# Two transformer layers on one core: four sets of expert weights in the first layer instead of two, some loaded earlier, and a copy moved in VectorE's order

## The chip, the core and the metric

The kernel runs on one core of a Trainium2 chip. The core has five engines that run their own instruction lists and meet at semaphores: TensorE (PE in the profile; PEld is its loading of weights), VectorE (DVE), ScalarE (ACT), GpSimd (POOL) and SyncE (SP), which here only issues transfers (DMA). Transfers are carried out by 16 DMA engines between the chip's memory (HBM) and the core's SBUF. Products land in PSUM. The metric is the device time of one execution in microseconds, as the median over runs.

## The reference

The input is x, 8 sequences of 100 rows of 256 values, and a context of 8 times 361 rows of 192. Two layers are applied; each adds a cross attention and then a feed-forward part. All arithmetic is in float32. What matters here is the feed-forward part of the first layer, which sends every row to one of 8 experts:

```python
def _L0_ffn_ref(x, Wg, bg, W1, b1, W2, b2):      # D_MODEL 256, D_HIDDEN 1024, 8 experts
    gate_scores = softmax(einsum('btd,de->bte', x, Wg) + bg)
    top1_mask = one_hot(argmax(gate_scores), 8)
    top1_weight = sum(gate_scores * top1_mask)
    h = silu(einsum('btd,edh->bteh', x, W1) + b1)
    o = einsum('bteh,ehd->bted', h, W2) + b2
    return sum(o * top1_mask[..., None], axis=2) * top1_weight

x = x + L0_xattn(layernorm(x), ctx_768, ...)      # 16 heads
x = x + L0_ffn(layernorm(x), ...)                 # the experts of this case
x = x + L1_xattn(layernorm(x), ctx_768, mask, ...)
x = x + L1_ffn(layernorm(x), ...)                 # 64 experts, top 8, and a shared one
```

## The kernel before

The kernel is written without a scheduler: each engine has its own program, a list of functions called in order at the end of `build`, and semaphores named after what is ready (`w1_loaded`, `rows_used`, `ys_ready`) order them against each other. An engine takes its instructions in the order written; one that waits holds up all behind it on the same engine.

The stages are, in the time of the profile: projections of the first attention (to 72 us), the first attention (to 200), the gate of the first feed-forward (to 217), its experts (to 324), the second attention with its projections, and the second feed-forward, which fills the rest.

**The gate and the dispatch.** `pe_gate` and `dve_gate` pick an expert for each of the 800 rows and compute a slot for it, so that the rows of one expert lie together, in blocks of 128. `pool_dispatch` writes the rows to `xs_dram` in that order by eight indirect transfers (L944). There are eight experts and, with these inputs, eleven blocks: one expert has four blocks and each other has one.

**The experts.** Every engine walks over the blocks with `each_block`, a loop over pairs of experts (L981). Its body is written out for the two members of the pair, p = 0 and 1. For each expert it has three copies of the block's code: for the first block, for the second, and one in an inner loop for the third and further ones, whose turns are tested one by one. The numbers of blocks are read from `per_expert_i` into registers.

In one block (`block` in `pe_experts`) TensorE multiplies the 128 rows by W1 of the expert (L1040: 16 products in two passes, 32 matmuls), transposes the rows of the next block (L1031, `take_rows`), and multiplies the hidden layer by W2 (L1053). ScalarE applies the bias and silu (L1082) and loads the rows of later blocks. VectorE copies the transposed rows of the next block out of PSUM (L1098, `take_rows`), copies the bias of the next expert (L1103), and adds b2 (L1106). SP stores the block's result in `ys_dram` (L1011).

**The weights.** One expert's W1 and W2 are 1 MB each. `w1_e` and `w2_e` have two buffers each, all four in the memory of the attention's values (`vals_arena`). SP loads the sets of experts 0 and 1 in `sp_experts`, which stands behind `sp_load1_weights`; that waits until the first attention has added its last result (`A0.added`) and then loads context and weights for the second attention. From then on SP loads the set of expert e+1 into the other buffer once TensorE has begun expert e (`expert_begun`). In SP's program this stands behind the store of the block before.

**Entrance of the experts.** VectorE's `dve_experts` first takes the transposed biases b1 out of PSUM (L1111), clears a row (L1112), copies the first expert's bias (L1114), and then copies the first rows (`take_rows(0)`, L1098). ScalarE's first silu waits for L1114, TensorE's first product for L1098. At the same time GpSimd splits the second attention's weights in two instructions (L1202).

The hidden layer `hT` and the broadcast b2 lie in the memory of the attention's keys (`keys_arena`). The first attention uses the first 5,776 of its 13,032 columns.

Of the kernel before, what the change touches and what calls it, by code (L numbers as in the profile page):

```python
# [13 lines left out]
P = 128  # L14
# [13 lines left out]
def build(nc, a):  # L28
# [82 lines left out]
    w1_e = [carve(vals_arena, at_v, (2, H0)) for _ in range(2)]  # L111
    w2_e = [carve(vals_arena, at_v, (HC, D)) for _ in range(2)]
# [4 lines left out]
    hT = carve(keys_arena, at_k, (HC, P))  # L117
# [4 lines left out]
    b2_all = carve(keys_arena, at_k, (E0, D))  # L122
# [146 lines left out]
    w1_loaded = [sem(f"w1_loaded{p}") for p in range(2)]  # L269
    w2_loaded = [sem(f"w2_loaded{p}") for p in range(2)]  # L270
# [703 lines left out]
    def each_block(e, run):  # L974

        def within(n):
            return nc.s_assert_within(n, 0, NBLK - 1, skip_runtime_bounds_check_because=
                                      "all experts take NBLK blocks at most")

        e.wait_ge(slots_ready, 1)  # L980
        with e.Fori(0, E0 // 2) as i:  # L981
            for p in range(2):
                blocks = e.value_load(per_expert_i[0:1, 0, bass.ds(2 * i + p, 1)], min_val=1, max_val=MAXB)
                first = e.value_load(per_expert_i[0:1, 1, bass.ds(2 * i + p, 1)], min_val=0, max_val=NBLK - 1)
                run(first, i, p, True)
                with e.If(blocks > 1):
                    run(within(first + 1), i, p, False)
                    with e.If(blocks > 2):
                        with e.Fori(2, MAXB) as k:
                            with e.If(blocks > k):  # L990
                                run(within(first + k), i, p, False)

    def sp_experts(sp):
        sp.dma_start(b1_rows[:, :], a["L0_ffn_b1"].rearrange("e (m q) -> (e m) q", q=P)).then_inc(biases_loaded, 16)
        sp.dma_start(b2_all[:, :, :], a["L0_ffn_b2"].rearrange("(o e) d -> o e d", o=1).broadcast_to([P, E0, D])
                     ).then_inc(biases_loaded, 16)
        def load(e, p):
            sp.dma_start(w1_e[p], a["L0_ffn_W1"].rearrange("e (c q) h -> q (e c) h", q=P)[:, bass.ds(2 * e, 2), :]
                         ).then_inc(w1_loaded[p], 16)
            sp.dma_start(w2_e[p], a["L0_ffn_W2"].rearrange("e (m q) d -> q (e m) d", q=P)[:, bass.ds(HC * e, HC), :]  # L1000
                         ).then_inc(w2_loaded[p], 16)

        def block(n, i, p, first):
            if first:

                with sp.If(i > 0 if p == 0 else i < E0 // 2 - 1):
                    sp.wait_ge(expert_begun, 2 * i + p + 1)
                    load(nc.s_assert_within(2 * i + p + 1, 1, E0 - 1, skip_runtime_bounds_check_because=
                                            "after the last expert there is none to load"), 1 - p)
# [3 lines left out]
        load(0, 0)  # L1013
        load(1, 1)
# [12 lines left out]
    def pe_experts(pe):  # L1027
# [6 lines left out]
        def block(n, i, p, first):  # L1034
# [12 lines left out]
            if first:  # L1047
                pe.wait_ge(w2_loaded[p], 16 * i + 16)
            pe.wait_ge(ys_ready, n + 1)
            for m in range(HC):  # L1050
                if m % 4 == 0:
                    pe.wait_ge(hidden_ready, 2 * n + 1 + m // 4)
                last = nc.tensor.matmul(ys_ps, hT[:, m, :], w2_e[p][:, m, :], start=(m == 0), stop=(m == HC - 1))  # L1053
# [18 lines left out]
    def act_experts(act):  # L1072
# [3 lines left out]
        def block(n, i, p, first):  # L1076
            if first:
                act.wait_ge(b1_ready, 2 * i + p + 2)
            for half in range(2):
                act.wait_ge(hidden_in_psum, 2 * n + half + 1)  # L1080
                for m in range(4 * half, 4 * half + 4):
                    last = nc.scalar.activation(hT[:, m, :], hid_ps[half][:, m % 4, :], ACT.Silu,  # L1082
                                                bias=b1_col[p][:, m:m + 1])
# [11 lines left out]
    def dve_experts(dve):  # L1095
# [4 lines left out]
        def block(n, i, p, first):  # L1100
            take_rows(n + 1)
            if first:
                nc.vector.tensor_copy(b1_col[1 - p], b1_all[:, bass.ds(2 * i + p + 1, 1), :]).then_inc(b1_ready, 1)  # L1103
            dve.wait_ge(ys_in_psum, n + 1)
            dve.wait_ge(ys_stored, 16 * n + 16)
            nc.vector.tensor_tensor(ys_rows, ys_ps, b2_all[:, bass.ds(2 * i + p, 1), :].rearrange("p e d -> p (e d)"),  # L1106
                                    ALU.add).then_inc(ys_ready, 1)

        dve.wait_ge(b1_in_psum, 1)
# [6 lines left out]
        take_rows(0)  # L1116
# [914 lines left out]
    with nc.Block() as block:  # L2031
        @block.sync
        def _(sp):
# [3 lines left out]
            sp_load_moe(sp)  # L2037
            sp_load1_weights(sp)
# [101 lines left out]
```

## Time and profile before

| | us |
|---|---|
| median of 3 runs | 796.9 (794.32 to 797.54) |
| profiled execution: span of its records | 799.0 |
| time around that span | not given |
| TensorE busy in the span | 702.9 (88%) |
| ScalarE busy | 413.8 (52%) |
| VectorE busy | 372.2 (47%) |
| GpSimd busy | 253.4 (32%) |
| SP's queue (q1): 58.40 MB | 23.6% of 16 engines' span |

The median is over unprofiled runs, the span is that of one profiled execution, and here it is the longer of the two. A line of the timeline gives the start, the time from the first to the last of the instructions merged in it, the engine, the line of the kernel, and in square brackets how long the engine had been idle before it and what ended that. SPq and ACTq are transfers being issued. Names of tiles are those of the memory they lie in: the experts' weights read `v_all`, their rows, hidden layer and biases `kT_all`.

### The profile page before, as it was taken

The numbers are of one execution on the slowest core, as the hardware profiler recorded it, in microseconds if no ns is written. First come the engines' busy times: TensorE is split into PE (matmuls) and PEld (weight loads), VectorE is DVE, ScalarE is ACT, GpSimd is POOL, SyncE is SP. The second block draws the span as 40 slices with busy tenths as digits, with TensorE's granted clock in tenths as the row PEclk, the third lists the DMA queues.
The fourth block names the chain that finished last, engine by engine and source line by source line (L and its number), as shares of the span: only waits on it lengthen the run. The fifth ranks groups of instructions, "written<-read, shape, count | busy, mean of one in ns | idle before, by whom it ended". The sixth has DMA issues, their size and how long they took to land.

```text
span 799.0 us, 15926 instructions
## 1 busy us (share of the span) xinstructions
PE 702.9 (88%) x4979; PEld 569.5 (71%) x4980; DVE 372.2 (47%) x1126; ACT 413.8 (52%) x966; POOL 253.4 (32%) x322
## 2 busy tenths in 40 slices
PE   3997999997539999699999899986799999999995
PEld 2775666665438898477666566655479999999995
DVE  4223577776421111476777555556843434242432
ACT  2445789987313332355556878763234444444442
POOL 5112455553160000211211000001236666666652
PEclk9998799999559999899999999996899999999999
DMA  5126000000835971100100100000044443344431
GB/s 134 42 82 199 1 2 2 2 3 1 295 119 182 301 247 33 54 24 19 38 19 0 46 2 1 2 1 1 0 132 131 129 120 122 121 122 120 129 112 41
DMA packets 58549, 62.51 MB, mean 78 GB/s; under 512 B 5920, under 2 KB 51206, under 8 KB 58378
## 3 DMA queue, kind: packets, MB, share of 16 engines
q1 hardware_dynamic: 55530, 58.40, 23.6%
q10 hardware_dynamic: 1952, 1.91, 0.8%
q0 software_dynamic: 1024, 1.64, 0.7%
q8 instruction: 25, 0.41, 0.2%
q14 instruction: 18, 0.15, 0.1%
HBM read 54.72 MB, written 7.22 MB: 78 GB/s over the span
## 4 chain that ended last, share of the span: by engine, by line
PE 68%; DVE 11%; ACT 9%; issue 5%; DMA 3%; POOL 3%; SPq 1%; DVEq 0%; POOLq 0%; ACTq 0%
PE psum L1876 6%; PE psum L1878 6%; PE psum L1877 5%; ACT probs L697 4%; PE psum L1040 4%; PE psum L1053 3%; PE psum L1395 3%; PE psum L1891 3%; PE psum L1892 3%; PE psum L545 3%; PE psum L1890 3%; PE psum L559 3%; PE psum L1416 3%; PE psum L636 3%; PE psum L1403 2%
## 5 line engine op out<-in xcount | busy, mean ns | idle before, releaser
L2000 DVE TENSOR_TENSOR kT_all<-kT_all 128x400 f32<-128x400 f32 x60 | 36.6, 611 | 114.5 <-ACT kT_all L1934 106.5
L1973 POOL TENSOR_TENSOR h_low<-v_all,h_high 128x400 fp32r<-128x400 f32 x60 | 63.1, 1051 | 65.5 <-ACT h_high L1938 65.4
L1876 PE MATMUL psum<-xT_high,we_high 128*128 128x400 f32 x240 | 83.3, 347 | 0.0
L1878 PE MATMUL psum<-xT_high,we_low 128*128 128x400 f32 x240 | 82.8, 345 | 0.0
L1877 PE MATMUL psum<-xT_low,we_high 128*128 128x400 f32 x240 | 82.5, 344 | 0.0
L697 ACT ACTIVATE probs<-probs,negmax 100x361 f32<-100x361 f32 x128 | 68.9, 587 | 10.8 <-POOL probs L742 10.7
L1964 POOL TENSOR_TENSOR we_low<-v_all,we_high 128x512 fp32r<-128x512 f32 (+1 forms) x61 | 66.6, 1101 | 19.6 <-ACT we_high L1923 16.0
L750 DVE TENSOR_SCALAR_CACHE_REDUCE probs<-psum 100x361 f32<-100x361 f32 x128 | 60.7, 531 | 19.5 <-PE psum L626 19.5
L636 PEld LDWEIGHTS psum<-ident,probs 100*128 100x128 f32 (+1 forms) x384 | 40.2, 159 | 27.6 <-issue 19.8
L636 PE MATMUL psum<-ident,probs 100*128 100x100 f32 (+1 forms) x384 | 48.7, 266 | 11.1 <-ACT probsT L705 4.8
L1934 ACT ACTIVATE kT_all<-psum 128x400 f32<-128x400 f32 x60 | 30.0, 501 | 52.7 <-PE psum L1878 52.7
L1082 ACT ACTIVATE kT_all<-psum,kT_all 128x128 f32<-128x128 f32 x88 | 25.2, 369 | 52.1 <-PE psum L1040 52.1
L742 POOL TENSOR_SCALAR probs<-probs 100x722 f32<-100x722 f32 x64 | 50.4, 788 | 5.0
L1040 PE MATMUL psum<-kT_all,v_all 128*128 128x128 f32 x352 | 44.4, 287 | 7.0 <-DMA v_all<-in_L_ffn_W_dram 2.8
L1040 PEld LDWEIGHTS psum<-kT_all,v_all 128*128 128x128 f32 x352 | 43.1, 202 | 9.7 <-issue 5.9
L1938 ACT ACTIVATE h_high<-v_all 128x400 fp32r<-128x400 f32 x60 | 32.2, 536 | 30.3 <-DVE v_all L2005 30.3
L1876 PEld LDWEIGHTS psum<-xT_high,we_high 128*128 128x128 f32 x240 | 45.1, 188 | 0.5 <-DVE v_all L2005 0.2
L1877 PEld LDWEIGHTS psum<-xT_low,we_high 128*128 128x128 f32 x240 | 45.2, 188 | 0.2
L1878 PEld LDWEIGHTS psum<-xT_high,we_low 128*128 128x128 f32 x240 | 45.1, 188 | 0.0
L950 POOL TENSOR_TENSOR ctxT_low<-ctxT_full,ctxT_high 96x722 fp32r<-96x722 f32 x9 | 15.4, 1709 | 88.6 <-ACT ctxT_high L1070 88.6
L1891 PE MATMUL psum<-h_high,we_high 128*128 128x400 f32 x120 | 41.4, 345 | 0.0
L1892 PE MATMUL psum<-h_low,we_high 128*128 128x400 f32 x120 | 41.3, 344 | 0.0
(350 smaller groups left out, 1566.7 us busy)
## 6 DMA issues: line engine op xcount, KB each, us to landing
v_all<-in_L_ffn_W_dram SPq DMA_DIRECT2D x16, 1024.0 KB, 7.7
kT_all<-coefT_dram SPq DMA_DIRECT2D x30, 400.0 KB, 3.5
v_all<-in_L_ffn_Wg_dram SPq DMA_DIRECT2D x31, 128.0 KB, 2.1
v_all<-in_L_ffn_Wu_dram SPq DMA_DIRECT2D x31, 128.0 KB, 2.2
v_all<-in_L_ffn_Wd_dram SPq DMA_DIRECT2D x31, 128.0 KB, 2.1
ctx_nat<-in_ctx_dram SPq DMA_DIRECT2D x17, 192.0 KB, 2.5
xs_dram<-zeros SPq DMA_DIRECT2D x1, 2048.0 KB, 7.7
ys_dram<-zeros SPq DMA_DIRECT2D x1, 1792.0 KB, 12.5
```

Source lines behind the costliest of these rows:

```text
L636: last = nc.tensor.transpose(pT_ps[0:rows[t], t, hh * NQ:(hh + 1) * NQ], probs[:, n % NPB, hh, t * P:t * P + rows[t]], ident[0:NQ, 0:NQ])
L697: last = nc.scalar.activation(row, row, ACT.Exp, bias=negmax[:, n % NPB, hh:hh + 1])
L742: nc.gpsimd.tensor_scalar(pair, pair, CLAMP, -CLAMP, ALU.min, ALU.max).then_inc(A0.clamped, 1)
L750: last = nc.vector.tensor_scalar(probs[:, n % NPB, hh, 0:NKV], psum[0:NQ, n % 2 * 2 + hh, 0:NKV], -CLAMP, None, ALU.max, ALU.max, accum_ou ...
L1040: last = nc.tensor.matmul(hid_ps[m // 4][:, m % 4, :], w1_e[p][:, c, m * P:(m + 1) * P], xsT[:, c, :], start=(c == 0), stop=(c == 1))
L1876: nc.tensor.matmul(ps, we_high[p][:, col], xT_high[:, c, tok], start=(c == 0), stop=False)
L1877: nc.tensor.matmul(ps, we_high[p][:, col], xT_low[:, c, tok], start=False, stop=False)
L1878: last = nc.tensor.matmul(ps, we_low[p][:, col], xT_high[:, c, tok], start=False, stop=(c == 1))
L1891: nc.tensor.matmul(ps, we_high[p][:, col], h1_high[p][:, tok], start=False, stop=False)
L1892: last = nc.tensor.matmul(ps, we_high[p][:, col], h1_low[p][:, tok], start=False, stop=False)
L1964: nc.gpsimd.tensor_tensor(we_low[p][:, cols], we[p][:, cols], we_high[p][:, cols].bitcast(F32), ALU.subtract).then_inc(we_split, 1)
L1973: nc.gpsimd.tensor_tensor(h1_low[p][:, tok], h1T[:, tok], h1_high[p][:, tok].bitcast(F32), ALU.subtract).then_inc(h1_ready, 1)
```

## The change

The weights get four sets of buffers (`BUFS0`). Two W1 and one W2 lie in the upper part of the keys' memory, which the first attention leaves unused; the others lie in the memory of the values. W2 is loaded in two halves. The hidden layer and b2 move to the memory of the queries. W1 and W2 of expert 0 and W1 of expert 1 are loaded by `sp_load_first_experts`, ahead of SP's wait for the end of the first attention; the second half of expert 1's set and the sets of experts 2 and 3 are loaded behind it. When expert e has begun, SP loads the set of expert e+3. The loop over the experts has a body for four experts and two turns. In `dve_experts`, `take_rows(0)` is the first instruction.

```diff
-    w1_e = [carve(vals_arena, at_v, (2, H0)) for _ in range(2)]
-    w2_e = [carve(vals_arena, at_v, (HC, D)) for _ in range(2)]
+    BUFS0, KT0 = 4, 2 * B * NKV
+    queries_arena = qT_all[:, :]
+    at_t, at_q = [KT0], [0]
+    w1_e = [carve(keys_arena, at_t, (2, H0)) for _ in range(2)]
+    w2_e = [[carve(keys_arena, at_t, (HC // 2, D)) for _ in range(2)]]
+    w1_e += [carve(vals_arena, at_v, (2, H0)) for _ in range(2)]
+    w2_e += [[carve(vals_arena, at_v, (HC // 2, D)) for _ in range(2)] for _ in range(2)]
+    w2_e.append([carve(vals_arena, at_v, (HC // 2, D)), vals_arena[:, 6 * SLOT_V + 2048:8 * SLOT_V].rearrange(
+        "p (m d) -> p m d", m=HC // 2)])
...
-    hT = carve(keys_arena, at_k, (HC, P))
...
-    b2_all = carve(keys_arena, at_k, (E0, D))
+    b2_all = carve(queries_arena, at_q, (E0, D))
+    assert at_k[0] <= KT0 and at_v[0] <= 6 * SLOT_V and at_t[0] <= 4 * (B + 1) * (NKV + 1)
...
-        with e.Fori(0, E0 // 2) as i:
-            for p in range(2):
-                blocks = e.value_load(per_expert_i[0:1, 0, bass.ds(2 * i + p, 1)], min_val=1, max_val=MAXB)
-                first = e.value_load(per_expert_i[0:1, 1, bass.ds(2 * i + p, 1)], min_val=0, max_val=NBLK - 1)
+        with e.Fori(0, E0 // BUFS0) as i:
+            for p in range(BUFS0):
+                blocks = e.value_load(per_expert_i[0:1, 0, bass.ds(BUFS0 * i + p, 1)], min_val=1, max_val=MAXB)
+                first = e.value_load(per_expert_i[0:1, 1, bass.ds(BUFS0 * i + p, 1)], min_val=0, max_val=NBLK - 1)
...
+    def load_w1(sp, e, p):
+        sp.dma_start(w1_e[p], a["L0_ffn_W1"].rearrange("e (c q) h -> q (e c) h", q=P)[:, bass.ds(2 * e, 2), :]
+                     ).then_inc(w1_loaded[p], 16)
+
+    def load_w2(sp, e, p):
+        src = a["L0_ffn_W2"].rearrange("e (m q) d -> q (e m) d", q=P)
+        for half in range(2):
+            sp.dma_start(w2_e[p][half], src[:, bass.ds(HC * e + half * (HC // 2), HC // 2), :]).then_inc(w2_loaded[p], 16)
+
+    def sp_load_first_experts(sp):
+
+        load_w1(sp, 0, 0)
+        load_w2(sp, 0, 0)
+        load_w1(sp, 1, 1)
+
     def sp_experts(sp):
+        load_w2(sp, 1, 1)
         sp.dma_start(b1_rows[:, :], a["L0_ffn_b1"].rearrange("e (m q) -> (e m) q", q=P)).then_inc(biases_loaded, 16)
         sp.dma_start(b2_all[:, :, :], a["L0_ffn_b2"].rearrange("(o e) d -> o e d", o=1).broadcast_to([P, E0, D])
                      ).then_inc(biases_loaded, 16)
         def load(e, p):
-            sp.dma_start(w1_e[p], a["L0_ffn_W1"].rearrange("e (c q) h -> q (e c) h", q=P)[:, bass.ds(2 * e, 2), :]
-                         ).then_inc(w1_loaded[p], 16)
-            sp.dma_start(w2_e[p], a["L0_ffn_W2"].rearrange("e (m q) d -> q (e m) d", q=P)[:, bass.ds(HC * e, HC), :]
-                         ).then_inc(w2_loaded[p], 16)
+            load_w1(sp, e, p)
+            load_w2(sp, e, p)
 
         def block(n, i, p, first):
             if first:
 
-                with sp.If(i > 0 if p == 0 else i < E0 // 2 - 1):
-                    sp.wait_ge(expert_begun, 2 * i + p + 1)
-                    load(nc.s_assert_within(2 * i + p + 1, 1, E0 - 1, skip_runtime_bounds_check_because=
-                                            "after the last expert there is none to load"), 1 - p)
+                with sp.If(i > 0 if p == 0 else i < E0 // BUFS0 - 1):
+                    sp.wait_ge(expert_begun, BUFS0 * i + p + 1)
+                    load(nc.s_assert_within(BUFS0 * i + p + BUFS0 - 1, BUFS0, E0 - 1, skip_runtime_bounds_check_because=
+                                            "after the last expert there is none to load"), (p - 1) % BUFS0)
             sp.wait_ge(ys_ready, n + 2)
             sp.dma_start(ys_dram[bass.ds(n * P, P), :], ys_rows).then_inc(ys_stored, 16)
 
-        load(0, 0)
-        load(1, 1)
+        for e in (2, 3):
+            load(e, e)
         each_block(sp, block)
...
-                pe.wait_ge(w2_loaded[p], 16 * i + 16)
+                pe.wait_ge(w2_loaded[p], 32 * i + 32)
...
-                last = nc.tensor.matmul(ys_ps, hT[:, m, :], w2_e[p][:, m, :], start=(m == 0), stop=(m == HC - 1))
+                last = nc.tensor.matmul(ys_ps, hT[:, m, :], w2_e[p][m // 4][:, m % 4, :], start=(m == 0), stop=(m == HC - 1))
...
-                act.wait_ge(b1_ready, 2 * i + p + 2)
+                act.wait_ge(b1_ready, BUFS0 * i + p + 2)
...
-                nc.vector.tensor_copy(b1_col[1 - p], b1_all[:, bass.ds(2 * i + p + 1, 1), :]).then_inc(b1_ready, 1)
+                nc.vector.tensor_copy(b1_col[1 - p % 2], b1_all[:, bass.ds(BUFS0 * i + p + 1, 1), :]).then_inc(b1_ready, 1)
...
+        take_rows(0)
         dve.wait_ge(b1_in_psum, 1)
         dve.wait_ge(biases_loaded, 32)
         nc.vector.tensor_copy(b1_all[:, 0:E0, :], b1_ps.rearrange("p (e m) -> p e m", e=E0))
...
         dve.sem_inc(ys_stored, 16)
-        take_rows(0)
         each_block(dve, block)
...
             sp_load_moe(sp)
+            sp_load_first_experts(sp)
             sp_load1_weights(sp)
             sp_experts(sp)
```

SP's program between the zero fills (L828) and the loop over the experts (L981), before: `ctx` is the context and `L1_xattn` the second attention's weights, ahead of them SP waits for the attention's end.

```order
L828 DMA ys_dram<-zeros 128x14x256
L429 DMA ctx_nat0<-in_ctx_768_dram 128x2x192
...
L1151 DMA early<-in_L1_xattn_Wq_dram 128x2x512
L994 DMA kT_all<-in_L0_ffn_b1_dram 64x128
L995 DMA kT_all<-in_L0_ffn_b2_dram 128x2048
L998 DMA v_all<-in_L0_ffn_W1_dram 128x2x1024
L1000 DMA v_all<-in_L0_ffn_W2_dram 128x8x256
L998 DMA v_all<-in_L0_ffn_W1_dram 128x2x1024
L1000 DMA v_all<-in_L0_ffn_W2_dram 128x8x256
L981 UNCONDITIONAL_BRANCH
```

The same stretch of SP's program, in the changed kernel:

```order
L836 DMA ys_dram<-zeros 128x14x256
L1002 DMA kT_all<-in_L0_ffn_W1_dram 128x2x1024
L1008 DMA kT_all<-in_L0_ffn_W2_dram 128x4x256 x2
L1002 DMA kT_all<-in_L0_ffn_W1_dram 128x2x1024
L437 DMA ctx_nat0<-in_ctx_768_dram 128x2x192
...
L1173 DMA early<-in_L1_xattn_Wq_dram 128x2x512
L1008 DMA v_all<-in_L0_ffn_W2_dram 128x4x256 x2
L1018 DMA kT_all<-in_L0_ffn_b1_dram 64x128
L1019 DMA qT_all<-in_L0_ffn_b2_dram 128x2048
L1002 DMA v_all<-in_L0_ffn_W1_dram 128x2x1024
L1008 DMA v_all<-in_L0_ffn_W2_dram 128x4x256 x2
...
L989 UNCONDITIONAL_BRANCH
```

Four loads (3 MB) now stand ahead of the wait and seven (5 MB, the last two like the two before them) behind it, where four of 1 MB each stood.

VectorE's program from the gate's last instruction to the loop over the experts, before:

```order
L907 CAST slot<-slot_f 100x8
L1111 COPY kT_all<-psum 128x64
L1112 MEMSET kT_all 128x8
L1114 COPY kT_all<-kT_all 128x8
L1098 COPY kT_all<-psum 128x256
L981 UNCONDITIONAL_BRANCH
```

And in the changed kernel:

```order
L915 CAST slot<-slot_f 100x8
L1120 COPY kT_all<-psum 128x256
L1134 COPY kT_all<-psum 128x64
L1135 MEMSET kT_all 128x8
L1137 COPY kT_all<-kT_all 128x8
L989 UNCONDITIONAL_BRANCH
```

The copy of the first rows (L1098, now L1120) has moved ahead of the three instructions on the biases; nothing else on VectorE changes its place.

## Rows read from the trace of the kernel before

**Rows 1.** Busy time by stretch; columns: length, engines' busy us, PEclk, DMA share, GB/s.
```profile
core 0: us, PE busy (x) PEld busy (x) DVE busy (x) ACT busy (x) POOL busy (x), PEclk, DMA share, GB/s
...
74.00:82.00 8.00, 5.37 (x28) 2.92 (x28) 3.93 (x17) 5.31 (x11) 4.03 (x8) 0.50 0.01 2
201.00:223.00 22.00, 10.20 (x58) 9.50 (x56) 7.44 (x31) 7.28 (x11) 4.81 (x5) 0.50 0.96 324
...
239.00:240.00 1.00, 1.00 (x8) 1.00 (x8) 0.00 (x0) 0.02 (x1) 0.00 (x0) 0.62 0.00 0
...
248.00:297.00 49.00, 45.61 (x306) 41.35 (x306) 6.00 (x19) 18.41 (x55) 0.00 (x0) 1.00 0.87 289
```

**Rows 2.** Timeline of TensorE, the first products of blocks (start, length).
```profile
234.06 6.54 PE L1040 MATMUL psum<-kT_all,v_all 128*128 128x128 f32 x32 [2.22 <-DVE kT_all L1098]
...
244.11 3.77 PE L1040 MATMUL psum<-kT_all,v_all 128*128 128x128 f32 x32
...
269.26 3.84 PE L1040 MATMUL psum<-kT_all,v_all 128*128 128x128 f32 x32 [1.08 <-DMA v_all<-in_L_ffn_W_dram]
...
277.33 3.81 PE L1040 MATMUL psum<-kT_all,v_all 128*128 128x128 f32 x32 [0.55 <-DMA v_all<-in_L_ffn_W_dram]
...
292.30 3.73 PE L1040 MATMUL psum<-kT_all,v_all 128*128 128x128 f32 x32
...
299.55 3.73 PE L1040 MATMUL psum<-kT_all,v_all 128*128 128x128 f32 x32
...
315.99 3.81 PE L1040 MATMUL psum<-kT_all,v_all 128*128 128x128 f32 x32 [1.79 <-issue]
```

**Rows 3.** The chain that ended last, 226 to 330 us.
```profile
247.64 0.42 SPq L998
248.27 8.83 DMA v_all<-in_L_ffn_W_dram
...
264.34 4.88 DMA v_all<-in_L_ffn_W_dram
```

**Rows 4.** Timeline of all engines where the experts begin.
```profile
226.26 0.99 POOL L944 DMA_INDIRECT xs_dram<-kT_all,slot  x1 [0.31 <-issue]
...
228.93 3.29 ACTq L1074 DMA_DIRECT2D kT_all<-xs_dram  x2
228.93 2.34 POOL L1202 TENSOR_TENSOR wk_low<-v_all,wk_high 96x1024 fp32r<-96x1024 f32 x1
...
229.51 0.23 DVE L1111 COPY kT_all<-psum 128x64 f32<-128x64 f32 x1 [12.88 <-PE psum L1061]
...
229.78 3.82 DVE L1114 COPY kT_all<-kT_all 128x8 f32<-128x8 f32 x1
...
231.15 0.69 PE L1031 MATMUL psum<-ident,kT_all 128*128 128x128 f32 x2 [1.68 <-DMA kT_all<-xs_dram]
231.23 2.34 POOL L1202 TENSOR_TENSOR wv_low<-v_all,wv_high 96x1024 fp32r<-96x1024 f32 x1
233.52 0.41 DVE L1098 COPY kT_all<-psum 128x256 f32<-128x256 f32 x1
234.02 1.28 ACT L1082 ACT_TABLE_LOAD   x1 [14.43 <-DVE kT_all L1114]
...
237.88 1.14 ACT L1082 ACTIVATE kT_all<-psum,kT_all 128x128 f32<-128x128 f32 x4 [2.58 <-PE psum L1040]
...
241.19 0.16 DVE L1103 COPY kT_all<-kT_all 128x8 f32 x1
```

**Rows 5.** Transfers from 256 to 325 us: queues, then issues.
```profile
q1 hardware_dynamic: 7736, 11.56, 50.2%
q10 hardware_dynamic: 1296, 1.18, 5.5%
...
kT_all<-xs_dram ACTq DMA_DIRECT2D x9, 128.0 KB, 5.4
```

**Rows 6.** Transfers from 234 to 256 us: the instruction queue.
```profile
q8 instruction: 2, 0.03, 0.6%
```

More of the change, by code:

```diff
@@ L116, in build @@
     xsT = carve(keys_arena, at_k, (2, P))
-    hT = carve(keys_arena, at_k, (HC, P))
+    hT = carve(queries_arena, at_q, (HC, P))
     ys_rows = carve(keys_arena, at_k, (D,))
@@ L268, in build @@
     xs_loaded, ys_in_psum, ys_stored = sem("xs_loaded"), sem("ys_in_psum"), sem("ys_stored")
-    w1_loaded = [sem(f"w1_loaded{p}") for p in range(2)]
-    w2_loaded = [sem(f"w2_loaded{p}") for p in range(2)]
+    w1_loaded = [sem(f"w1_loaded{p}") for p in range(4)]
+    w2_loaded = [sem(f"w2_loaded{p}") for p in range(4)]
     xsT_ready = sem("xsT_ready")
@@ L1082, in block @@
                     last = nc.scalar.activation(hT[:, m, :], hid_ps[half][:, m % 4, :], ACT.Silu,
-                                                bias=b1_col[p][:, m:m + 1])
+                                                bias=b1_col[p % 2][:, m:m + 1])
                 last.then_inc(hidden_ready, 1)
@@ L1102, in block @@
             if first:
-                nc.vector.tensor_copy(b1_col[1 - p], b1_all[:, bass.ds(2 * i + p + 1, 1), :]).then_inc(b1_ready, 1)
+                nc.vector.tensor_copy(b1_col[1 - p % 2], b1_all[:, bass.ds(BUFS0 * i + p + 1, 1), :]).then_inc(b1_ready, 1)
             dve.wait_ge(ys_in_psum, n + 1)
             dve.wait_ge(ys_stored, 16 * n + 16)
-            nc.vector.tensor_tensor(ys_rows, ys_ps, b2_all[:, bass.ds(2 * i + p, 1), :].rearrange("p e d -> p (e d)"),
+            nc.vector.tensor_tensor(ys_rows, ys_ps, b2_all[:, bass.ds(BUFS0 * i + p, 1), :].rearrange("p e d -> p (e d)"),
                                     ALU.add).then_inc(ys_ready, 1)
+        take_rows(0)
         dve.wait_ge(b1_in_psum, 1)
```

## The prediction, made before the changed kernel was run

> **What bounds the kernel now.** I read the page's slices first, then a table of stages, then the stretch from 196 to 323 us instruction by instruction, then the chain of waits. Reference times are those of the trace before the change, in us from the start of the span.
>
> The table of stages [rows 1] shows three things. The transfer engines stand still in the first attention (share 0.01 from 74 to 82). They are full right behind it (0.96 from 201 to 223, at 324 GB/s), while TensorE is busy with the gate for 10.20 of 22.00 us at a granted clock of 0.50, that is 1.2 GHz. And in the experts (248 to 297) TensorE is busy 45.61 of 49.00 us at the full clock with the transfers at 0.87 beside it. So TensorE bounds the experts, and what is to be had there is its idle time.
>
> How much that is comes from the starts of the blocks of 128 rows, each of which opens with the 32 matmuls of L1040 [rows 2]. Where no weights are loaded a block takes 299.55 - 292.30 = 7.25 us. From 244.11 to 292.30 there are six blocks in 48.19 us, and six clean ones are 43.50: 4.69 us are lost. The chain of waits says to what: it runs through the weights' transfers before experts 2, 4 and 6 [rows 3] (a third one, of the same length as the second, stands before expert 6). The reason stands in the code. With two sets, the set of expert e+1 can be loaded only once expert e has begun and SP has stored the block before it.
>
> One more gap, 1.79 us before 315.99 [rows 2], is called issue. It follows the only expert with four blocks, whose inner loop still has three empty turns to test. The change keeps that loop, so I keep the gap.
>
> The other loss is at the entrance [rows 4]. The first 128 rows land, TensorE transposes them from 231.15 to 231.84, and VectorE copies the result only at 233.52. It was in the bias copy L1114 from 229.78 for 3.82 us. A copy of the same shape takes 0.16 at 241.19. What ends when L1114 ends (233.60) is GpSimd's second subtraction (231.23 + 2.34 = 233.57): the two shared something, and the small copy stood behind it.
>
> **The change, part by part.**
>
> *Rows ahead of the biases.* In VectorE's program the copy of the rows moves ahead of L1111, L1112 and L1114. It waits for the transposes alone, which end at 231.84, 1.68 us ahead of its start now. With a little for the handover it gains 1.6. Would GpSimd hold this copy too? Its source is PSUM. The nearest row is L1111, also from PSUM, which took 0.23 us at 229.51 beside the first subtraction [rows 4]. It has 64 columns instead of 256, so the bounds are 0 (held like L1114) and 1.6; I take 1.6. The bias copies then end as before at about 233.6, because GpSimd sets that. What is late next: ScalarE waits for them, then loads its table (1.28 us, from 0.42 after L1114's end), so it is ready at 235.3. The first half of the hidden layer now comes 3.82 us (237.88 - 234.06) after 232.46, at 236.3. So the table is hidden, with 1.0 us to spare.
>
> By the Trainium skill (SBUF — State Buffer, Who interferes with whom), GpSimd holds the port pair that it shares with VectorE for a whole instruction, and a VectorE instruction with at most one SBUF input outside the 2-port modes never wants it. By that rule the gain is the full 1.6; had the copy read SBUF it would be 0.
>
> *The clock at that place.* The first block ran at 0.50 until about 239.8 (the slice from 239 to 240 has 0.62, [rows 1]). Its 32 matmuls took 6.54 against 3.73 at the full clock [rows 2]; at 0.50 all the way they are 7.46. If the clock rises as long after the start as before, 5.7 us, the whole 1.6 stays. If it rises at the same instant, the matmuls take from 232.46 to 239.8 and not to 240.6, and 0.8 stays. If it rises after some 4 us, the matmuls take 4.0 + (7.46 - 4.0)/2 = 5.7, and 2.4 are gained. I take 1.6.
>
> *Four sets of weights.* The waits in the six blocks go if the weights are there in time. Sets 0 to 3 are all asked for before the experts begin, sets 4 to 7 when experts 1 to 4 begin. Expert 1 would begin at about 242.5, and SP gets to its load 3.5 us behind that (247.64 against 244.11 before, [rows 2, 3]), at 246.0. The set needs 9.5 us from there (248.27 + 8.83 = 257.10, less 247.64), so set 4 is there at 255.5; expert 4 starts three blocks after expert 1, at 264.3. Sets 5 and 6 follow a block apart. From 248 to 297 six sets with their rows took 0.87 of 49 us [rows 1], 7.1 us each, so they just keep up with 7.25. The gain is the 4.69 less what is no wait for weights: a loop that turns back once instead of three times still has to read its registers. The matmuls behind such a turn take 3.84 and not 3.73 at 269.26 and 299.55 [rows 2]; I leave 0.2 for the one turn. Bounds: 4.7 above; below, 3.8, if what the chain doesn't name stays: 0.82 before 277.33 (277.33 - 269.26 - 7.25) and 0.1 behind expert 6's start. I take 4.5, since the 0.82 lies in the first block of a set too.
>
> *One and a half sets loaded early.* SP's program now has four loads (3 MB) behind the zero fills and ahead of its wait for the attention's end; SP has nothing else there, so nobody waits for SP. The transfers would fill 74 to 83 us, where the engines were at 0.01. What could they slow down? In the experts L1040 took 3.73 beside full transfers at 292.30 and 3.73 at 299.55 beside none, and 3.81 to 3.84 behind a gap [rows 2]. So 0, with 0.5 as the upper bound (3% of the eight us, twice).
>
> *Two and a half sets behind the attention.* Before, 4 MB of expert weights went there, now 5 MB. The extra MB takes 3.2 us at 324 GB/s. The transfers run full until 223 [rows 1], now until about 226. SP issues them later too, but is first wanted at 245. The biases, now behind half a set, still land long ahead of 229.51, where VectorE takes them. The scatter of the rows on GpSimd ends at 227.25 and shares the engines. Its last piece is issued at 226.26, when the extra MB is nearly through, and the reading of the rows starts at 228.93 [rows 4]. Cost between 0 and 3.2; I take 0.3, near the end at which GpSimd's own issue sets the pace.
>
> *hT and b2 in the queries' memory, weights of the second layer in two halves:* same instructions and sizes. The buffers are free there since the first attention is over. 0.
>
> *Code.* The loop over the experts has four bodies and two turns instead of two and four. In 234 to 256 the trace has 2 instruction transfers, and in 256 to 325 none, though the loop turned back twice [rows 5, 6]. So code that was there stays there. I take 0, for the new bodies too, which are reached by jumps forward like the second body in the first turn: no gap before 244.11.
>
> **Sum.** 1.6 + 4.5 - 0.3 = 5.8 us, all of it on the chain, since the chain leaves the experts through the last block's store and gather. Against the profiled execution: 799.0 - 5.8 = 793.2 for the span. What lies around its span is not shown, and the median of the runs, 796.9, is even below the span, so I take the difference from the median: 791.1 us.
>
> **Rivals.**
>
> *Code, on the slower side.* The gap of 1.79 is not the loop's tests but the fetch of the next expert's code, and with double the code every change of expert pays it. For it: the gap is called issue, and it stands at a jump to another copy. Against it: at 244.11 such a jump costs nothing, and no instruction transfer stands in 256 to 325 [rows 5, 6]. It would be 6 further gaps, 10.7 us, less the 5.8: 796.9 + 4.9 = 801.8. It turns the sum from the fourth gap on.
>
> By the Trainium skill (Runtime: NRT & Kernel Launch, Instruction fetch mechanics) a taken branch whose target is outside a window of two pages stalls until the page is fetched; it puts pages at 16 KiB. By that rule this rival would be the forecast. The trace does not agree as far as two bodies go, since the turns in 256 to 325 fetched nothing; for four bodies no row shows it.
>
> *The waits come back.* The loads of sets 4 to 6 press on the engines together with the rows (5.4 us to landing there, [rows 5]) and the block stores behind them in SP's queue, and TensorE waits about 1 us in each of four blocks: 796.9 - 5.8 + 4 = 795.1. Against it: the transfers have a slack of nine us on set 4, and some four on set 6.
>
> *Only the waits go.* GpSimd holds the new first copy as well: 796.9 - 4.2 = 792.7.
>
> **How the numbers follow.** Forecast 0.66, with a range of its own from 788.5 to 793.5: the clock's instant gives 0.9 either way, the scatter up to 1.5, and further falls and rises of the clock behind the experts shift with the work. Only the waits 0.12; the waits come back 0.13; code 0.06; 0.03 is left for the rest. A measurement here tells 0.5% (4 us, about the 3.2 between the three runs) from no change. Faster than 792.9 is most of the forecast and half of "only the waits": 0.66. Within 0.5%: 0.28. Slower: 0.06. The range 787.5 to 796.5 leaves out the code and the far ends.
>
> **What would show it.** Right: the copy of the rows starts within 0.1 us of the transposes' end, no matmul of the experts waits for a transfer, blocks are 7.25 us apart from the second to the seventh, and the stage ends at about 317 instead of 323.1. The first attention lasts as before, with the transfers full from 74 to 83. Wrong: waits called issue at experts 2, 3 or 4 with instruction transfers beside them (code), the first copy held until 233.5, the reading of the first rows more than a microsecond behind GpSimd's last scatter (the extra MB), or weights in the chain again.

## The result, and the profile after

The changed kernel takes 802.6 us, the median of 4 runs (802.12 to 803.3), against 796.4 for the kernel before on the same chip: a ratio of 1.0081, with a 95% interval from 1.0065 to 1.0096. It is slower by 6.2 us, where 5.8 us were to be gained. Its profiled execution took 803.0 us with a span of 801.0 us, so some 2.0 us lie around a span. The profiled execution of before had a span of 799.0 us: with as much around it, that execution was a long one, some 4.6 us above its median. Spans of the two are therefore not compared below; stretches inside the experts are.

The starts of the blocks on TensorE (L1062, which was L1040) answer to [rows 2]. The columns are start, length, engine, line, tiles, and in brackets the idle time before it.

```profile
232.70 6.63 PE L1062 MATMUL psum<-kT_all 128*128 128x128 f32 x32 [1.35 <-DVE kT_all L1120]
...
242.84 3.76 PE L1062 MATMUL psum<-kT_all 128*128 128x128 f32 x32
...
250.11 1.28 PE L1062 MATMUL psum<-kT_all,v_all 128*128 128x128 f32 x10
253.96 2.61 PE L1062 MATMUL psum<-kT_all,v_all 128*128 128x128 f32 x22 [2.57 <-issue]
...
265.55 5.60 PE L1062 MATMUL psum<-kT_all,v_all 128*128 128x128 f32 x32 [5.30 <-issue]
...
275.00 3.83 PE L1062 MATMUL psum<-kT_all 128*128 128x128 f32 x32 [0.17 <-issue]
...
289.58 3.73 PE L1062 MATMUL psum<-kT_all,v_all 128*128 128x128 f32 x32
...
296.83 3.73 PE L1062 MATMUL psum<-kT_all,v_all 128*128 128x128 f32 x32
```

No wait for weights is left, as predicted. In their place stand a gap of 2.57 us inside the block of expert 2 and one of 5.30 us ahead of expert 3, both called issue. From 242.84 to 296.83 six blocks take 53.99 us, and six clean ones 43.50: 10.49 us are lost, where it was 4.69. From 289.58 on the blocks are 7.25 us apart.

The chain of waits (start, us, what) answers to [rows 3]: it goes through the gaps.

```profile
251.39 2.57 issue
...
260.25 5.30 issue
```

The long gap has a second price. These are busy times by stretch, with the columns of [rows 1]. After the gap TensorE ran its 32 matmuls in 5.60 us and not 3.73, with a granted clock of 0.50, that is 1.2 GHz. TensorE had been idle since 260.25, and the clock was already at 0.50 in the stretch from 262.5.

```profile
253.00:262.00 9.00, 6.29 (x40) 5.52 (x39) 0.93 (x3) 2.29 (x8) 0.00 (x0) 1.00 0.90 299
262.50:269.00 6.50, 3.46 (x16) 3.48 (x17) 0.00 (x0) 0.00 (x0) 0.00 (x0) 0.50 0.18 32
270.00:276.00 6.00, 5.83 (x38) 5.07 (x37) 0.93 (x3) 2.91 (x7) 0.00 (x0) 1.00 0.79 279
```

The transfers of instructions answer to [rows 6]. First from 240 to 275 us, and then in the two gaps alone, 251 to 254 and 260.3 to 265.6 (queue: packets, MB, share):

```profile
q8 instruction: 5, 0.08, 1.0%
...
q8 instruction: 1, 0.02, 2.2%
...
q8 instruction: 2, 0.03, 2.8%
q14 instruction: 2, 0.02, 0.9%
```

Five pieces of 0.016 MB are fetched in the first turn of the loop, where two were before; one lies in the short gap and two in the long one. From 275 to 325 us q8 moves nothing. That q8 carries TensorE's code is seen in the runs below: where TensorE's program alone is changed, the count on q8 changes with it. The long gap also has two small transfers on q14; the gap of 8.80 us in the kernel with unused code, below, has none on q14, so such a gap does not need them.

The entrance, on all engines, answers to [rows 4]:

```profile
224.92 0.99 POOL L952 DMA_INDIRECT xs_dram<-kT_all,slot  x1 [0.30 <-issue]
...
228.56 3.18 ACTq L1096 DMA_DIRECT2D kT_all<-xs_dram  x2
...
230.66 0.69 PE L1053 MATMUL psum<-ident,kT_all 128*128 128x128 f32 x2 [2.53 <-DMA kT_all<-xs_dram]
...
231.39 0.42 DVE L1120 COPY kT_all<-psum 128x256 f32<-128x256 f32 x1 [16.10 <-PE psum L1053]
```

The copy starts right behind the transposes, as it should. But the first product comes at 232.70, 0.89 us after the copy's end: from the transposes' start to it are 2.04 us instead of 2.91, so 0.87 us are gained, not 1.6. And ScalarE reads the rows 3.64 us after the last scatter's start, where it was 2.67; the transposes start 5.74 us after it, where it was 4.89.

### The profile page after: what moved, and what is told of

The parts are those of the page before. It is cut to its first block, busy times and chain, and to the rows that moved or that the text cites. A ratio compares the mean times of both kernels' runs of the same rounds, so it can differ in the third digit from the quotient of the medians.

```text
span 801.0 us, 15892 instructions
## 1 busy us (share of the span) xinstructions
PE 701.8 (88%) x4979; PEld 570.0 (71%) x4980; DVE 367.4 (46%) x1126; ACT 411.3 (51%) x964; POOL 253.7 (32%) x322
## 4 chain that ended last, share of the span: by engine, by line
PE 69%; DVE 11%; ACT 9%; issue 5%; POOL 2%; DMA 1%; DVEq 0%; POOLq 0%; ACTq 0%; SPq 0%
PE psum L1062 6%; PE psum L1898 6%; PE psum L1900 5%; PE psum L1899 5%; PE psum L1075 5%; ACT probs L705 4%; PE psum L553 3%; PE psum L1913 3%; PE psum L1914 3%; PE psum L1912 3%; PE psum L567 3%; PE psum L1417 3%; PE psum L1438 2%; PE psum L1425 2%; PE psum L644 2%
## 5 line engine op out<-in xcount | busy, mean ns | idle before, releaser
L705 ACT ACTIVATE probs<-probs,negmax 100x361 f32<-100x361 f32 x128 | 68.9, 587 | 10.3 <-POOL probs L750 10.0
L1104 ACT ACTIVATE qT_all<-psum,kT_all 128x128 f32<-128x128 f32 x88 | 25.2, 369 | 62.7 <-PE psum L1062 62.7
L1912 PE MATMUL psum<-h_high,we_low 128*128 128x400 f32 x120 | 41.1, 343 | 0.0
L1800 POOL TENSOR_TENSOR xT_low<-kT_all,xT_high 128x1600 fp32r<-128x1600 f32 x1 | 3.6, 3559 | 118.7 <-ACT xT_high L1779 118.7
```

Source lines behind the costliest of these rows:

```text
L705: last = nc.scalar.activation(row, row, ACT.Exp, bias=negmax[:, n % NPB, hh:hh + 1])
L1912: nc.tensor.matmul(ps, we_low[p][:, col], h1_high[p][:, tok], start=False, stop=False)
```

## The experiments

What is compared throughout: the time; "lost", which is what six blocks from the second block's start take above 43.50 us; and "scatter to read", from the start of GpSimd's last scatter to the start of ScalarE's reading of the rows.

**The kernel before, once more.**

> The kernel before, profiled once more: a control, with no edit. Its first profiled execution had a span of 799.0 us and its own time some 4.6 us above the median of its timed runs. Theory A (that execution was an unlucky one, by the phase of the clock in attention): the span is now 793 to 796 us, and the waits for weights (six blocks, 4.69 us in all) are there again within 1 us. Theory B (a profiled execution always costs this): the span is 798 to 800 us again.

It took 793.9 us with a span of 792.1 us. Six blocks went from 240.79 to 288.90 us, 4.61 us lost, and scatter to read took 2.69. The span is that of theory A, and the two stretches repeat within 0.1 us, so the first profile's long span is not theirs. That the clock in the attention made it long was not followed up. From the first transposes to the first product it was 3.09 us here, against 2.91 in the first profile.

**VectorE's rows first, alone.**

```diff
+        take_rows(0)
         dve.wait_ge(b1_in_psum, 1)
...
-        take_rows(0)
         each_block(dve, block)
```

> The kernel before with one edit: the copy of the first rows stands ahead of the bias copies on VectorE. The trace of the changed kernel shows the copy starting right behind its transposes, but the first expert product only 2.04 us after the transposes began, with 0.88 us called issue behind the copy. Theory F (a new floor: TensorE's own register reads of the loop take that long after the transposes): the first product starts 2.04 us after the transposes began, where before it was 2.91, so the stage gains 0.9 us and the median 0.5 to 1.2. Theory P (the prediction's term): 1.6 us, with the product 1.3 us behind the transposes. Rival: the extra weights had delayed TensorE in the changed kernel, not the register reads; then the product starts within 1.4 us here too.

It took 795.1 us (12 runs), a ratio of 0.9984 with an interval from 0.9967 to 1.0001. From its timeline of TensorE and VectorE:

```profile
228.82 0.69 PE L1031 MATMUL psum<-ident,kT_all 128*128 128x128 f32 x2 [1.67 <-DMA kT_all<-xs_dram]
230.96 5.94 PE L1040 MATMUL psum<-kT_all,v_all 128*128 128x128 f32 x32 [1.44 <-DVE kT_all L1098]
...
229.55 0.42 DVE L1098 COPY kT_all<-psum 128x256 f32<-128x256 f32 x1 [15.24 <-PE psum L1031]
...
230.16 1.14 DVE L1115 COPY kT_all<-kT_all 128x8 f32<-128x8 f32 x1
```

The first product comes 2.14 us behind the transposes' start, though the copy is done 1.17 us behind it. In both kernels with the new order some 0.9 to 1.0 us lie between the copy's end and the product. In that place TensorE's program has only the entry into the loop, with its register reads; this says where the time is, and no run took the reads away. The bias copy again ends with GpSimd's second subtraction (231.30 and 231.26), which hurts nobody now. The edit is worth 0.8 to 0.95 us (against 2.91 and 3.09 in the two profiles of before), too little for the timed runs to show beyond doubt.

**Code that never runs, in the kernel before.** Three more copies of the block's code stand at the end of each of TensorE's two bodies, under a condition that is never true. TensorE has about as much loop code as in the changed kernel; buffers, loads and order are those of before.

```diff
+                if unused:
+                    with e.If(blocks > MAXB - 1):
+                        for _ in range(unused):
+                            run(first, i, p, False)
...
-        each_block(pe, block)
+        each_block(pe, block, unused=3)
```

> The kernel before, two sets and two bodies, with three more copies of a block's code in TensorE's program at the end of each body, under a test (more than 6 blocks) that is never true here. Nothing more is executed but the test. Theory C (the gaps of the changed kernel are the first fetch of code that a jump lands in): the second body now begins about twice as far behind the first, so a gap called issue of 2.5 to 5.5 us stands at expert 1 for the first time, with an instruction transfer beside it, none from expert 2 on, and the kernel is 2 to 7 us slower. Theory T (the gaps come from the registers and tests of a four-body loop, or from the weights): no gap there, and a time within 1 us of before.

It took 810.4 us, a ratio of 1.0171 (1.0138 to 1.0204): 14.2 us slower than before, by code that does nothing. Its timeline of TensorE:

```profile
245.44 3.81 PE L1044 MATMUL psum<-kT_all,v_all 128*128 128x128 f32 x32 [2.92 <-issue]
...
261.72 5.37 PE L1044 MATMUL psum<-kT_all,v_all 128*128 128x128 f32 x32 [8.80 <-issue]
...
270.64 3.81 PE L1044 MATMUL psum<-kT_all,v_all 128*128 128x128 f32 x32
...
326.29 5.43 PE L1044 MATMUL psum<-kT_all,v_all 128*128 128x128 f32 x32 [2.01 <-issue]
```

Its transfers of instructions, from 238 to 262 us and in the long gap alone (252.9 to 261.7):

```profile
q8 instruction: 5, 0.08, 1.2%
...
q8 instruction: 3, 0.05, 2.1%
```

Five pieces again, three of them in the gap of 8.80 us: 2.93 us each. One of the other two lies in the gap of 2.92 us. From 262 to 325 us there is none, and no such gap at the later experts; only the gap behind the expert with four blocks is 2.01 us, and 32 matmuls behind it take 5.43 us where they took 3.81 before. That code costs was expected, and the gap at expert 1 too. The size (2 to 7 us) was not, because a gap of 8.80 us stands at expert 2 as well, where the loop turns back for the first time and none was expected. The six blocks lose 13.44 instead of 4.69 us; with 2.92 ahead of them and 1.62 behind the last gap that is 13.3 of the 14.2 us.

**The loop's code walked over before it is needed.** The changed kernel with one more turn of TensorE's loop ahead of the first rows; in it every expert is jumped over.

```diff
+        with e.Fori(0, E0 // BUFS0 + 1) as t:
+            for p in range(BUFS0):
+                with e.If(t > 0):
...
+            with e.If(t < 1):
+                entry()
```

> The changed kernel, with one turn more of the loop in TensorE's program, run while TensorE waits for the scatter: in it a test at each body's start jumps over the body, so that the places where the bodies begin are touched once; the first rows are transposed at its end. Theory C: the gaps of 2.57 us in expert 2 and 5.30 us before expert 3, and the 1.87 us that the fallen clock cost behind them, go for the most part, the instruction transfers move to 217 to 230 us, and the kernel takes 7 to 10 us less than the changed one, about 793 to 795. If only the first page of each body is touched and the later ones are still missing, the gap of 2.57 inside expert 2's products stays. Theory T: the gaps stay where they are, and the time is that of the changed kernel, 802.6.

It took 795.9 us (10 runs), 0.9985 of before (0.9963 to 1.0006), and 6.8 us less than the changed kernel, just under the 7 to 10 that were expected. Its transfers of instructions from 217 to 234 us, and then its timeline of TensorE:

```profile
q8 instruction: 5, 0.08, 2.3%
```

```profile
232.73 0.34 PE L1109 MATMUL psum<-ident,kT_all 64*128 64x64 f32 x1 [16.11 <-issue]
...
235.46 5.25 PE L1087 MATMUL psum<-kT_all 128*128 128x128 f32 x32 [1.77 <-issue]
...
251.52 3.73 PE L1087 MATMUL psum<-kT_all,v_all 128*128 128x128 f32 x32
...
258.77 3.73 PE L1087 MATMUL psum<-kT_all,v_all 128*128 128x128 f32 x32
...
312.24 5.46 PE L1087 MATMUL psum<-kT_all,v_all 128*128 128x128 f32 x32 [1.88 <-issue]
```

All five pieces now come before the experts, q8 moves nothing from 234 to 325 us, and 0.74 us of the six blocks are lost instead of 10.49. That it only draws level with before has its reason in the first row, for the most part: the walk holds TensorE until 232.73, and the first product comes 2.8 us later than in the changed kernel. The last row adds 1.65 us: behind the gap of 1.88 us the 32 matmuls take 5.46 us, where they take 3.81 behind the changed kernel's 1.79.

**Two copies of the block's code instead of three.** The changed kernel; on TensorE the second block of an expert goes through the inner loop too.

```diff
                 with e.If(blocks > 1):
-                    run(within(first + 1), i, p, False)
-                    with e.If(blocks > 2):
-                        with e.Fori(2, MAXB) as k:
+                        with e.Fori(1, MAXB) as k:
```

> The changed kernel, with two instead of three copies of the block's code in each of TensorE's four bodies (the second block of an expert is run by the inner loop as well). The jump from one body to the next passes over one copy instead of two. Theory C: shorter jumps land in code that is nearer, so the 5.30 us before expert 3 shrink to 2.6 or less and the clock does not fall there; the time is 3 to 8 us under the changed kernel's 802.6. Theory T (tests and registers): one more turn of tests for each expert with more than one block, no gain, 802.6 or a little more.

It took 792.3 us (8 runs), a ratio of 0.9945 (0.9922 to 0.9967): faster than before, and 10.3 us under the changed kernel, more than the 3 to 8 expected. In its timeline of TensorE nothing waits from the second block to the eighth, be it for weights or for code:

```profile
242.91 3.75 PE L1067 MATMUL psum<-kT_all 128*128 128x128 f32 x32
...
250.19 3.81 PE L1067 MATMUL psum<-kT_all,v_all 128*128 128x128 f32 x32
...
257.51 3.73 PE L1067 MATMUL psum<-kT_all,v_all 128*128 128x128 f32 x32
...
264.96 3.83 PE L1067 MATMUL psum<-kT_all 128*128 128x128 f32 x32
...
286.80 3.73 PE L1067 MATMUL psum<-kT_all,v_all 128*128 128x128 f32 x32
```

0.39 us of the six blocks are lost, of which 0.20 lie at the loop's turn (257.51 to 264.96 is 7.45). Three pieces of code still come from 240 to 275 us, and nothing waits for them:

```profile
q8 instruction: 3, 0.05, 0.6%
```

The entrance is worse than in the changed kernel, though nothing was changed there (GpSimd's and ScalarE's rows): scatter to read is 4.61 us. Why it is longer than the changed kernel's 3.64, with the same transfers asked for, stays open.

```profile
224.79 0.99 POOL L952 DMA_INDIRECT xs_dram<-kT_all,slot  x1 [0.30 <-issue]
...
229.40 3.21 ACTq L1101 DMA_DIRECT2D kT_all<-xs_dram  x2
```

**Two sets of buffers, one and a half loaded early.** The changed kernel with `BUFS0` = 2 and without the loads of sets 2 and 3 ahead of the loop. It keeps the new places in memory, the early loads and the new order.

```diff
-    BUFS0, KT0 = 4, 2 * B * NKV
+    BUFS0, KT0 = 2, 2 * B * NKV
...
-        for e in (2, 3):
-            load(e, e)
```

> The changed kernel, but with two sets of weights buffers instead of four; the early loads and VectorE's rows first stay. Expected by the theory (turns that land on code not yet loaded cost 9.7 us, four sets gain 4.7): no bodies for the third and fourth set, so no gap of 2.6 or 5.3 us at experts 1 and 2; the waits for weights of the kernel before come back (4 to 5 us in six blocks); first product 2.1 us behind the row transposes' start; 794 to 796 us, 7 us below the changed kernel. Rival (the memory layout or the early loads themselves slow something): 798 us or more with no gap at the experts' turns.

It took 797.2 us (10 runs), 0.9992 of before (0.9972 to 1.0012). No gap called issue is left at experts 1 to 6, and the waits for weights are back:

```profile
250.54 3.84 PE L1060 MATMUL psum<-kT_all 128*128 128x128 f32 x32 [1.14 <-DMA kT_all<-in_L_ffn_W_dram]
...
255.91 3.72 PE L1073 MATMUL psum<-kT_all,qT_all 128*128 128x256 f32 x16 [1.32 <-DMA kT_all<-in_L_ffn_W_dram]
...
268.00 3.84 PE L1060 MATMUL psum<-kT_all 128*128 128x128 f32 x32 [1.13 <-DMA kT_all<-in_L_ffn_W_dram]
```

The six blocks lose 5.55 us and not 10.49. The median lies 5.4 us below the changed kernel and 1 us above what was expected; its interval reaches that. So the early loads by themselves gain nothing: what limits two sets is the loading of the next expert's.

**How much is queued behind the attention.** Two kernels, both with two copies of the code. In the first, set 3 is asked for when expert 0 has begun, and 3 MB of expert weights stand behind the attention instead of 5. In the second, nothing is loaded early, and it is 8 MB.

```diff
-        for e in (2, 3):
-            load(e, e)
+        load(2, 2)
...
-                with sp.If(i > 0 if p == 0 else i < E0 // BUFS0 - 1):
+                with sp.If(i < (E0 // BUFS0 if p == 0 else E0 // BUFS0 - 1)):
```

```diff
-            sp_load_first_experts(sp)
             sp_load1_weights(sp)
+            sp_load_first_experts(sp)
```

> The kernel of e4_two_copies (two copies of the block's code, 792.3 us) with the fourth set's first load put to expert 0's beginning, so that less is queued behind the attention while GpSimd's scatter and ScalarE's read of the rows go on. Theory D (the extra traffic delays the rows by 1 to 2 us): the rows are read 1.5 to 2.5 us after the last scatter's issue instead of 3.6, and the time falls to 790 to 791 us. Rival (that delay is by chance, or the fourth set comes too late for expert 3): 792 to 793 us, or a new wait at expert 3's first block.

> The kernel of e4_two_copies, but the first one and a half sets are loaded behind the attention too, so that four whole sets (8 MB) are queued there instead of 5. Theory D: the weights' traffic lasts some 9 us longer, the rows are read 4 us or more after the last scatter's issue, and the first expert's weights, which are first in their queue, still come in time; 793.5 to 797 us. Rival (the queued megabytes don't matter to the scatter and the rows): the same 792.3 us as e4_two_copies within 0.7 us.

They took 790.5 us (6 runs; ratio 0.9913, 0.9887 to 0.9939) and 797.8 us (10 runs; 0.9999, 0.9978 to 1.0020). The first lies in its expected range, though the rows are read 2.69 us behind the last scatter and not 1.5 to 2.5; the second lies 0.8 us above its range. ScalarE's reading and the transposes with 3 MB (the last scatter started at 224.41):

```profile
227.10 3.06 ACTq L1100 DMA_DIRECT2D kT_all<-xs_dram  x2
...
229.08 0.69 PE L1057 MATMUL psum<-ident,kT_all 128*128 128x128 f32 x2 [1.46 <-DMA kT_all<-xs_dram]
```

And with 8 MB (the last scatter started at 224.37):

```profile
230.48 6.58 ACTq L1101 DMA_DIRECT2D kT_all<-xs_dram  x2
...
235.99 0.69 PE L1058 MATMUL psum<-ident,kT_all 128*128 128x128 f32 x2 [8.41 <-DMA kT_all<-xs_dram]
```

All kernels side by side; the DMA share is that of the 2.7 us from the last scatter's start:

| kernel | MB behind attention | DMA share | scatter to read, us | lost in six blocks, us | time, us |
|---|---|---|---|---|---|
| before | 4 | 0.27 | 2.67 | 4.69 | 796.4 |
| before again | 4 | 0.27 | 2.69 | 4.61 | 793.9 |
| rows first | 4 | 0.29 | 2.69 | 5.07 | 795.1 |
| unused code | 4 | 0.26 | 2.69 | 13.44, and 2.92 ahead | 810.4 |
| two sets | 1 | 0.26 | 2.68 | 5.55 | 797.2 |
| changed | 5 | 0.71 | 3.64 | 10.49 | 802.6 |
| walked first | 5 | 0.73 | 5.02 | 0.74 | 795.9 |
| two copies | 5 | 0.77 | 4.61 | 0.39 | 792.3 |
| two copies, set 3 later | 3 | 0.26 | 2.69 | 0.37 | 790.5 |
| two copies, none early | 8 | 1.04 | 6.11 | 0.38 | 797.8 |

Up to 4 MB the rows are read 2.67 to 2.69 us behind the last scatter in every kernel; with 5 MB it is 3.6 to 5.0 us, and with 8 MB 6.1. With 8 MB the rows also take longer to arrive: the transposes start 11.62 us behind the last scatter, against 6.75 in the kernel with two copies, 5.74 in the changed one and 4.67 with 3 MB. Loading 3 MB early is worth 4 to 5.5 us: 4.87 at the transposes, 5.5 between the medians (792.3 against 797.8), and 4.3 by the ratios, since the two were compared with the kernel before on different chips. With four sets, that is what the early loads are for. Whether set 3 later gains in the time as well is less sure: 2.1 us at the transposes and 1.8 between the medians, with overlapping intervals. Its row of the entrance is clear, and it has the lowest median of all.

## Why the prediction was wrong

**The step that failed** is the last one of the sum: "Code ... I take 0, for the new bodies too, which are reached by jumps forward like the second body in the first turn". The change's loop makes TensorE fetch five pieces of code in its first turn where it was two, and three of these are waited for. The six blocks lost 10.49 us where I had put 0.2: 2.57 and 5.30 in the gaps, 1.87 by the clock that fell in the longer one, 0.17 and some register reads at the loop's turn. That is 10.3 of the 12.0 us between the gain of 5.8 forecast and the loss of 6.2 measured. Two runs show the cause from both sides. Unused code in the kernel before brings such gaps without any other change, and fewer copies in the changed kernel take them away with everything else kept. A third, the walk, keeps all the code and takes the gaps away by having it fetched before.

The reading of the trace was not false: code that had been there did stay. In the changed kernel q8 fetched nothing from 275 us to the end of the loop, and in no kernel did it fetch anything in the later turns. The error was to carry it over to code that had not been there yet. The evidence for 0 was one jump (244.11) in a loop of two bodies. The slower rival named the right resource, and its 801.8 us lies near the 802.6 measured, but not for its reason: it charged 1.79 us at each of six changes of expert, while the runs show two gaps, both in the first turn. The 1.79 us behind the expert with four blocks is there in every kernel (1.77 to 2.01) and is no part of this. A chance of 0.06 was too little for the one cost that the trace of before could not show. By the Trainium skill (Runtime: NRT & Kernel Launch, Instruction fetch mechanics) a taken branch to code outside the pages at hand stalls until it is fetched. The gap of 5.30 us ahead of expert 3, with its two transfers, agrees with that. The gap of 2.57 us does not stand at a jump: it opens after ten of 32 matmuls that follow each other in the program. The same section gives both a window of two pages and, for TensorE, a larger instruction memory of 128 KiB. Five pieces of 0.016 MB served the later turns without another fetch, which does not agree with a window of two pages and does agree with 128 KiB.

**Rows ahead of the biases: right in the mechanism, too large.** The copy is not held by GpSimd (0.42 us from 231.39, beside the subtraction that runs from 229.90 for 2.34 us), and it starts at once. But 1.6 us supposed that the first product follows the copy as closely as before (0.54 us from start to start). With the copy early, TensorE's own entry into the loop is late next, and 0.87 us are gained; the order alone gave 0.77 to 0.95 (2.91 and 3.09 to 2.14). Missed by 0.7 us.

**Four sets of weights: right.** No wait for weights is left in any kernel with four sets. Where two copies of the code leave no wait for it, the six blocks lose 0.37 to 0.39 us, so the term is 4.3 us against 4.5, and the loop's turn costs the 0.2 that was set aside.

**Two and a half sets behind the attention: too small.** I took 0.3 of bounds from 0 to 3.2. It was 0.97 us in the changed kernel and 1.94 in the one with two copies, which has the same transfers. The argument that the extra MB is nearly through at the last scatter's issue was the weak point: in the 2.7 us from the last scatter's start the transfers stand at 0.71 instead of 0.27, and that is when the scattered rows must land. Missed by 0.7 us here (0.55 by the start of the transposes). The three misses are 11.7 of the 12.0 us.

**One and a half sets loaded early: right.** The loads run from 64.7 us, and the transfers are at 1.04 from 74 to 82 us where they were at 0.01; TensorE was busy 5.06 us there (5.37 before) and 100.14 us from 86 to 200 (101.28 before), at granted clocks of 0.55 and 0.99 (0.50 and 0.98).

The forecast of 791.1 us was thus, by its own terms, that of a kernel in which the code and the queue cost nothing. A kernel without these two costs exists: two copies, set 3 later, 790.5 us. It beats both the kernel before and the changed one. That it lands so near the forecast is in part luck: the terms as measured, 4.3 for the weights and 0.9 for the rows, are 5.2 of the 6.4 us between its median and that of the kernel before beside it, and the rest was not traced.

## What to carry to other kernels

Code is a buffer too: where a change writes out a loop's body more often, count the fetches of instructions in the first turn, not in a later one, and see whether a copy can be merged away before more buffers are added. A stretch of the trace without fetches only says that the code run in it was there already. And a prefetch that is moved ahead must be followed to whoever shares the transfer engines with its tail: here one more megabyte delayed the small indirect transfers behind which everything stood, and asking for one set later freed them.

## What the runs showed of the hardware

A wait for code costs about as much for each piece of 16 KB fetched in it: 2.57 and 2.92 us with one, 5.30 with two, 8.80 with three. The transfer itself is less than half of that: 2.2% of 16 engines over 3 us is 1.06 us for one piece, and 2.1% over 8.8 us is 2.96 us for three. What the rest is, no run shows. Not every fetch is waited for: the kernel with two copies fetched three pieces between 240 and 275 us without a gap. Which jumps of the changed kernel meet code that is not there, and why the gap at expert 2 opens after ten of its 32 matmuls, was not settled.

TensorE kept five such pieces over the later turns of its loop, in the changed kernel, with unused code and with the walk.

Behind the gap of 5.30 us 32 matmuls took 5.60 us instead of 3.73, at a granted clock of 0.50. So that wait cost a third more than it lasted. Behind the gap of 2.57 us they went on at full speed (22 in 2.61 us). The length of the gap alone does not tell which it will be. Behind the expert with four blocks, 1.79 us of idle time in the changed kernel were followed by matmuls at 1.00 (320.6 to 324.3). With the walk 1.88 us were followed by 0.50 (314 to 316), and with unused code 2.01 us by 0.50 (326.5 to 329), and the 32 matmuls there took 5.46 and 5.43 us.
